# The second pair of waits taken out of GpSimd's gathers in an attention layer over edges

## What is computed

```python
w_m = (efeat @ W_msg + b_msg).reshape(E, in_f, -1)
w_a = (efeat @ W_attn + b_attn).reshape(E, in_f, -1)
h_src = feat[src][:, :, None]
e1 = w_m * h_src
e2 = w_a * h_src
seg_max = jax.ops.segment_max(e2, dst, num_segments=N)
ex = jnp.exp(e2 - seg_max[dst])
denom = jax.ops.segment_sum(ex, dst, num_segments=N)
attn = ex / denom[dst]
ft = jax.ops.segment_sum(e1 * attn, dst, num_segments=N)
return ft.sum(axis=1)
```

## Time and profile before

| | |
|---|---|
| median of 3 runs | 6410.05 us (6404.79 to 6413.98) |
| the profiled execution | 6405.31 us, span 6403.6 us |
| busy: PE, DVE, ACT, POOL | 2752.5, 3554.8, 1211.0, 4012.1 us |
| mean granted clock of TensorE | 0.71 of 2.4 GHz |
| gathers of the attention layer | 1695 with a mean of 1157 ns |

### The profile page before, as it was taken

The page is one execution under the profiler, slowest core; times in us unless marked ns, Lnnn a source line. Parts: engine busy times, 40 slices in busy tenths (PEclk is TensorE's granted clock), DMA queues, the critical chain, the costliest instruction groups (busy, mean ns, idle before and its releaser), DMA issues.

```text
span 6403.6 us, 57451 instructions
## 1 busy us (share of the span) xinstructions
PE 2752.5 (43%) x13527; PEld 1931.1 (30%) x13528; DVE 3554.8 (56%) x4214; ACT 1211.0 (19%) x1559; POOL 4012.1 (63%) x3713
## 2 busy tenths in 40 slices
PE   3530000000000000000367788777778788778777
PEld 1110000000000000000145555555556555556555
DVE  8321112121222122233468888888888888888887
ACT  3440000000000000000122222222222222222222
POOL 0325766767676676675466666666666666677663
PEclk9965555555555555555678888988888888888888
DMA  5861111111111111111000001001001011011110
GB/s 159 270 212 18 20 26 26 23 31 25 28 33 27 27 30 30 33 39 31 20 13 20 20 20 28 20 20 27 21 20 28 20 28 28 20 28 28 28 28 18
DMA packets 157958, 251.68 MB, mean 39 GB/s; under 512 B 73726, under 2 KB 130563, under 8 KB 145156
## 3 DMA queue, kind: packets, MB, share of 16 engines
q0 software_dynamic: 126192, 100.10, 8.0%
q1 hardware_dynamic: 31711, 151.31, 7.1%
q10 hardware_dynamic: 32, 0.01, 0.0%
HBM read 113.57 MB, written 136.63 MB: 39 GB/s over the span
## 4 chain that ended last, share of the span: by engine, by line
PE 22%; issue 21%; DVEq 18%; POOL 16%; DVE 14%; DMA 5%; another core or an unknown queue 2%; POOLq 1%; ACT 1%; SPq 0%; ACTq 0%
POOL gath L350 15%; PE psS L555 8%; PE psS L560 7%; DVEq L1193 5%; PE psW L549 4%; DMA table<-arena 3%; DVE stage L1154 3%; DVEq L1161 3%; DVE stage L1196 2%; DVEq L1121 2%; DVE work L756 1%; DVE arena L1154 1%; DVEq L1154 1%; POOL info_dram L321 1%
## 5 line engine op out<-in xcount | busy, mean ns | idle before, releaser
L350 POOL DMA_INDIRECT gath<-h_dram,hidx x1695 | 1961.2, 1157 | 1051.3 <-issue 550.1
L350 POOL DMA_INDIRECT gath<-table,blkidx x1646 | 1621.2, 985 | 535.8 <-issue 506.4
L543 PE MATMUL psT<-identb,stage 128*100 128x128 bf16 x2448 | 228.0, 252 | 2530.0 <-issue 2461.4
L560 PE MATMUL psS<-stage,ident 128*128 128x256 f32 x3390 | 936.0, 432 | 166.6 <-DVE stage L1196 161.0
L543 PEld LDWEIGHTS psT<-identb,stage 128*100 128x100 bf16 x2448 | 204.6, 152 | 2568.6 <-issue 2528.8
L555 PE MATMUL psS<-arena,ident 128*128 128x256 f32 x3390 | 829.1, 382 | 0.2 <-issue 0.2
L1154 DVE TENSOR_TENSOR arena<-psW,gath 128x768 f32 (+1 forms) x565 | 522.4, 952 | 529.9 <-DMA gath<-h_dram,hidx 293.5
L560 PEld LDWEIGHTS psS<-stage,ident 128*128 128x128 f32 x3390 | 710.6, 217 | 320.7 <-DVE stage L1196 199.0
L549 PE MATMUL psW<-wst,stage 100*128 100x256 bf16 x3390 | 577.1, 291 | 308.4 <-DVE arena L1154 171.5
L555 PEld LDWEIGHTS psS<-arena,ident 128*128 128x128 f32 x3390 | 605.4, 191 | 70.4 <-issue 0.4
L692 ACT ACTIVATE arena<-arena 128x1536 f32<-128x1536 f32 (+1 forms) x294 | 421.8, 1435 | 984.9 <-DVE arena L1183 983.7
(11 more groups left out here) (222 smaller groups left out, 2478.0 us busy)
## 6 DMA issues: line engine op xcount, KB each, us to landing
table<-arena SPq DMA_DIRECT2D x50, 1610.0 KB
ef<-arena SPq DMA_DIRECT2D x50, 805.7 KB
gath<-h_dram,hidx POOLq DMA_INDIRECT x1695
gath<-table,blkidx POOLq DMA_INDIRECT x1646
arena<-in_edge_attr SPq DMA_DIRECT2D x50, 257.8 KB
table<-arena SPq DMA_DIRECT2D x50, 186.9 KB
arena<-first_dram POOLq DMA_DIRECT2D x1, 915.5 KB, 13.7
info<-info_dram POOLq DMA_DIRECT2D x2, 432.0 KB, 6.4
```

The lines of the kernel that those rows point to most:

```text
L350: pool.indirect_dma_start(out=gath[:, q, s, :], out_offset=None, in_=rows, in_offset=bass.IndirectOffsetOnAxis(ap=idx[:, q, s:s + 1].bitca ...
L543: last = nc.tensor.transpose(psTb[0:KE, t % 2, j, 0:GP], efs[:, 8 * t + j, :], identb[0:GP, 0:GP])
L560: nc.tensor.matmul(psS[0:GP, IO:2 * IO], ident[0:GP, 0:GP], prod[:, c0:c0 + IO], start=False, stop=False)
```

## The change

GpSimd no longer waits before halves 6 and 8. The waits before halves 1, 2 and 4 stay, and so do all other engines' instructions. The branches for 6 and 8 in `pace` are then called by nothing.

```diff
                     for b in range(MINH, NHW):
                         with pool.If(nh > b):
-                            if b in (6, 8):
-                                if q:
-                                    pace(k, b, done)
-                                else:
-                                    with pool.If(i > 0):
-                                        pace(k, b, done)
                             gather(h2_d, hidx, q, b, HALF, hgath)
```

## The result

The changed kernel takes 6437.1 us (median of 20 runs), the kernel before 6410.1 us beside it (20 runs): ratio 1.0039, 95% interval 1.0031 to 1.0048. It is 27 us slower where 16 us less was forecast. The 20 runs of the changed kernel spread from 6404.8 to 6455.7 us, those of the kernel before from 6404.3 to 6424.2. The profiled execution took 6425.4 us, with a span of 6423.7, so it shows a smaller loss than the median.

A forecast was written before the change was run, and what follows sets the result against it. No engine alone bounds the attention stage; waits between engines decide. Window 2's 4.7 us, 8.7 from seven windows, 2.0, 0.35 and 0.3 make 16.1 us off 6410.0: 6394, range 6380 to 6404.

The forecast's parts named there:

- The mechanism of the gathers: Attention stage: GpSimd's waits for L1196 (179.1 us) go; gathers starting inside L1196 are held until 0.82 us after it ends.
- Rival (b): Attention stage: gathers are not held, so the waits come back whole, 128 us, giving 6282; chance 0.03.
- The lead of 1.25 us: Windows 3 to 24: the last gather ends 1.25 us earlier (1.64 in 14), for about 5.99 us of waits removed.
- Rival (c): Gathers lock to VectorE's blocks with a lead of three gathers instead of one: 38 us, giving 6372; chance 0.06.
- The sum of the gains: Attention stage, all windows together: 16.1 us gained, 0.25%, from 6410.0 to 6394.
- The clipping by TensorE: Windows 3 to 23: TensorE limits the 1.25 us lead to 1.0 in 11 and 13, 0.35 in 4, 0.15 or 0 later.
- the bound of 28.4: Upper bound if TensorE clips nothing: 19 windows give 1.25 us each, plus 4.7 in window 2, 28.4 us (6382).
- Windows 25 to 49: 0: Late attention windows: no gain, though 4.9 us of waits go in each of windows 27, 29, 31 and 33.
- window 2's 4.7: Window 2: removed waits of 6.06 and 2.72 us become a 4.7 us lead, since window 1 before it is short.
- Rival (d): Attention stage: TensorE's clock makes ten windows slower, 31 us lost against 16.1 won, 6425; chance 0.04 beyond 0.2%.
- C: Later theory of the 27 us loss: moving the gathers shifted TensorE's clock and the order of work.
- S: Later theory: back-to-back GpSimd gathers limit other engines needing instructions not at hand to one per 0.70 us; GpSimd waits relieve.

The follow-up runs named there:

- before_again: The kernel before, word for word, on chip 8, which shows no stalls: 6177.9 us, ratio 1.0002.
- after_again: The changed kernel, word for word, on chip 8, which shows no stalls: 6150.6 us, ratio 0.9957 to the kernel before.
- q0_again: Changed kernel with the waits before halves 6 and 8 kept for even windows' gathers only, on chip 5: 6400.7 us, ratio 0.9988 to the kernel before.
- q1_again: Changed kernel with the waits before halves 6 and 8 kept for odd windows' gathers only, on chip 5: 6453.4 us, ratio 1.0061 to the kernel before.
- breath: Changed kernel with three small GpSimd memsets and drains in place of each removed wait, on chip 5: 6548.1 us, ratio 1.0209 to the kernel before.
- mid_free: Kernel before with the waits before halves 6 and 8 removed for gathers of windows 3 to 23 alone, on chip 5: 6507.5 us, ratio 1.0075.
- pause: Changed kernel with seven small GpSimd memsets and drains in place of each removed wait, on a chip without stalls: 6439.7 us, ratio 1.0424.
- first_layer_breath: Changed kernel with even windows' waits kept, plus three memsets and drains in each of 50 first-layer steps, chip without stalls: 6508.0 us, ratio 1.0548.

## Why the prediction was wrong

**The mechanism of the gathers: right.** GpSimd's waits for L1196 are gone, the mean of L350 rose from 1157 to 1223 ns, and GpSimd's busy time from 4012.1 to 4125.8 us for the same work. The rule of the held gather stands: a gather of the changed kernel under the L1190 of 3528.82 (1.76 us) is held until 0.82 us after its end,

```profile
3528.95 2.44 POOL L350 DMA_INDIRECT gath<-h_dram,hidx  x1 [0.30 <-issue]
```

3528.95 + 2.44 = 3531.39, and 3528.82 + 1.76 + 0.82 = 3531.40. By the inference of the Trainium skill ("SBUF — State Buffer", "Who interferes with whom") that the writing of descriptors is not held by such an instruction, it would have ended at 3529.9. In the kernel before all 197 gathers that start inside an L1196 are held in this way, and in the changed kernel all 251 inside an L1190. Rival (b), which rests on it, is out.

**The lead of 1.25 us: right.** Window 5 waited 9.38 us before and 8.10 in the changed kernel, 1.28 less. In before_again the last gather of window 5 ends 7.07 us after the last L1196 of window 4, in after_again 5.82 us. Rival (c), three gathers of lead, is out. For windows 27 to 33 it is 0.82 us in both, no lead, as said.

**The sum of the gains: 4 us too low on chips without stalls.** Windows 3 to 23 gave 19.1 us for 11.4. The clipping by TensorE was costed too strictly: up to the start of window 14 it is 15.5 us for 11.05 (window 4 alone gave 1.3 for 0.35), behind it some 3.5 for 0.3. Window 2 gave 0.9 for 4.7, since the 6.06 us wait from which the 4.7 was worked out is 3.74 us longer than in before_again, 2.56 of them VectorE's own stall. That the total came near is in part luck: the two misses point opposite ways. In all 20.3 us of the stage for 16.1, within the bound of 28.4.

**"Windows 25 to 49: 0", and window 2's 4.7: the steps that failed.** They took a wait of GpSimd to be a cost alone, and everything behind it to move up or stay. On the chip of the recorded pair these windows lost 26.8 us, and window 1's messages, which the change does not touch, grew by 33.7. No semaphore makes VectorE's messages wait for the gathers of the next window, and I looked for no other tie in that direction. q0_again, q1_again and breath showed that there is one: with the gathers of even windows in one unbroken train window 1 takes 73.4 us, with a wait or a pause in them 39.6 or 39.7. I asked what holds GpSimd, and never what GpSimd holds.

**Rival (d), slower: the right sign by the wrong cause.** TensorE's granted clock from 3116 to 6400 us is a mean 0.86 in the recorded profiles of both kernels. The means over the whole execution, 0.926 after and 0.71 before, differ by the first layer, where TensorE does little: from 300 to 2900 us its clock is 1.00 of 2.4 GHz after and 0.51 before. And the time doesn't follow them: the changed kernel's 11 runs at 0.69 to 0.71 have a median of 6438.1 us, its 9 at 0.92 to 0.93 one of 6435.6. That settles the clock part of C too.

**It could have been seen.** VectorE's waits in the kernel before held the sign of it: 392.9 us of "issue" ahead of L963 and 321.2 ahead of L998 in the first layer, in instructions of 0.2 us that wait for nothing. In before_again they are 99.1 and 70.1 us. I skipped them because the change is in the other stage. In window 1 the L1154 of 3240.61 stood 2.56 us for "remote" and went on 2.5 us after GpSimd had stopped.

**What stays open.** S as it is worded, with the issuing of gathers as the cause, does not fit all of the record. In the first layer of the kernel before, GpSimd stands 26 times for 2.6 to 39 us, and in 23 of these stands the 0.70 us go on, up to 15 us behind the last gather. GpSimd, then VectorE:

```profile
833.26 0.95 POOL L350 DMA_INDIRECT gath<-table,blkidx  x1 [0.30 <-issue]
842.71 0.95 POOL L345 DMA_INDIRECT blkidx<-pairp,bst  x1 [8.50 <-remote]
```

```profile
838.44 0.16 DVE L963 SCALAR_TENSOR_TENSOR bstf<-tabs,info 128x1 f32 x1 [10.94 <-issue]
839.84 0.16 DVE L964 SCALAR_TENSOR_TENSOR rem<-tabs,info 128x1 f32 x1 [1.24 <-issue]
841.24 0.15 DVE L966 TENSOR_SCALAR bst<-bstf 128x1 int32<-128x1 f32 x1 [1.24 <-issue]
```

So a wait of GpSimd helps the messages of odd windows, as the runs show, but it does not end the slow pace everywhere. Why instructions come at 0.70 us on one chip and not on three others is not shown, nor by what way GpSimd's gathers get in between; that it is the fetching of instructions is argued, from the load on SyncE, from three engines standing at once and from VectorE's empty queue with its weights ready. Why only the odd windows suffer is open too: both kinds run the same operations, written out one behind the other in each loop. Where the code lies in memory was not shifted alone, as the moves meant for that were dropped; but mid_free, q0_again and breath are three differently built programs, and up to window 33 each is healed just where its waits or pauses are. The size varies for one and the same program: the changed kernel lost 0.4% in the recorded pair, and 1.4 and 0.5% on chip 5.

## What to carry to other kernels

A wait that looks like pure loss on an engine off the path may be what gives the other engines room on some chips; when you take it out, look through the profile for engines that stand for "issue" or "remote" while that engine works without a pause, in every stage, not just the changed one. Before trusting a change of half a percent, time it on more than one chip: here its sign turns between two of them. If the room is needed, keep the wait at the places that need it (half of these waits sufficed) and don't buy it with a pause of its own.

## What the runs showed of the hardware

- The kernel before took 6169 to 6178 us on three chips and 6410 to 6450 on chip 5 and in the recorded pair. 170 us of it lie in the first layer, where engines take one instruction per 0.70 us in the recorded traces and VectorE one per 0.13 us on chip 8 (2332.12), while GpSimd issues an indirect DMA every 1.25 us.
- The 0.70 us are shared: two engines that crawl together take one instruction per 1.40 us each, on one common grid (820.18 to 823.69 in the kernel before).
- On chip 5 a load of nothing but satisfied waits on SyncE cost 22 us beside a GpSimd that pauses, and 148 us beside one that doesn't.
- GpSimd stands 1.3 to 7.3 us behind the first memset of a pause (breath and pause, median 2.1; first_layer_breath 1.9 to 6.4, median 5.2), where only a drain stands, though the memset takes 0.33 us.
- An indirect DMA of GpSimd that starts inside a VectorE tensor_tensor with both inputs in SBUF ends 0.82 us after that instruction (197 of 197 beside L1196 before); beside L1154 or L1183, with one input in PSUM, it takes its 0.95 us.
